# A graph network on one core: target degrees from run ends by rounds of eight largest keys, and loads of edge ends in three pieces

## The reference

```
h   = relu(layernorm(x))
x   = x + gnn(h)        # message = mlp(h[src], edge_attr), averaged over the edges of a target, then a second mlp
h   = relu(layernorm(x))
x   = x + propagate(h)  # ten steps; feat0 = h
    f   = f * clip(out_deg, 1)**-0.5
    agg = segment_sum(f[src], dst)
    f   = 0.9 * agg * clip(in_deg, 1)**-0.5 + 0.1 * feat0
```

## Time and profile before

| | us |
|---|---|
| three runs: lowest, median, highest | 8115.39, 8118.78, 8119.13 |
| profiled execution, its own time | 8119.95 |
| its span, first to last instruction | 8118.4 |
| TensorE (PE) busy | 5850.0 (72%) |
| VectorE (DVE) busy | 4429.2 (55%) |
| GpSimd (POOL) busy | 1670.8 (21%) |
| ScalarE (ACT) busy | 737.9 (9%) |

### The profile page before, as it was taken

The page is one execution under the profiler, slowest core; times in us unless marked ns, Lnnn a source line. Parts: engine busy times, 40 slices in busy tenths (PEclk is TensorE's granted clock), DMA queues, the critical chain, the costliest instruction groups (busy, mean ns, idle before and its releaser), DMA issues. The chain is left out here.

```text
span 8118.4 us, 215578 instructions
## 1 busy us (share of the span) xinstructions
PE 5850.0 (72%) x86684; PEld 3701.6 (46%) x86684; DVE 4429.2 (55%) x12772; ACT 737.9 (9%) x1743; POOL 1670.8 (21%) x1737
## 2 busy tenths in 40 slices
PE   5924444444444444443879999999999999999998
PEld 4723333333333333332435465556554655555555
DVE  4744444444444444443376666666666666666665
ACT  0012222222222222221100000000000000000000
POOL 0044444444444444445000000000000000000000
PEclk9986666666666666666589999999999999999999
DMA  2022222222222222221045555555555555555554
GB/s 80 0 66 60 60 60 64 60 60 61 62 60 60 60 60 60 63 60 51 4 180 193 201 191 199 193 201 191 200 193 201 192 201 193 193 197 198 202 193 173
DMA packets 442509, 1013.57 MB, mean 125 GB/s; under 512 B 253086, under 2 KB 371838, under 8 KB 387262
## 3 DMA queue, kind: packets, MB, share of 16 engines
q1 hardware_dynamic: 386878, 968.76, 33.6%
q0 software_dynamic: 54912, 33.89, 2.3%
HBM read 838.71 MB, written 176.58 MB: 125 GB/s over the span
## 5 line engine op out<-in xcount | busy, mean ns | idle before, releaser
L1529 PE MATMUL banks_fast<-count_units_fast,feature_parts_fast 128*32 128x512 fp8e3 x70608 | 3823.6, 379 | 50.3 <-DVE count_units_fast L1424 46.4
L1529 PEld LDWEIGHTS banks_fast<-count_units_fast,feature_parts_fast 128*32 128x32 bf16 x70608 | 2048.6, 97 | 1801.9 <-issue 54.1
L1423 DVE TENSOR_SCALAR count_units_fast<-packed_ring_fast 128x512 int32<-128x512 int32 x2949 | 1257.8, 427 | 1424.1 <-PE banks_fast L1529 1391.4
L858 POOL DMA_INDIRECT rows_fast<-row_table,idx_fast x1568 | 1508.8, 962 | 968.1 <-DVE idx_fast L939 489.8
L1117 PE MATMUL banks_fast<-w1a_b1a_fast,turn_fast 49*128 49x96 f32 x3136 | 372.5, 374 | 1815.5 <-ACT turn_fast L1028 1589.2
L1424 DVE TENSOR_SCALAR count_units_fast<-packed_ring_fast 128x512 int32<-128x512 int32 x2949 | 1240.3, 421 | 0.0
L1117 PEld LDWEIGHTS banks_fast<-w1a_b1a_fast,turn_fast 49*128 49x128 f32 x3136 | 293.3, 259 | 1913.7 <-ACT turn_fast L1028 1499.6
L963 DVE TENSOR_TENSOR window_src_hot_fast<-iota_by_windows_fast,window_keys_fast 128x1024 bf16<-128x1024 bf16 x392 | 270.3, 690 | 1585.5 <-PE banks_fast L1089 920.7
L967 DVE TENSOR_SCALAR window_place_hot_fast<-iota_wide_fast,local_keys_fast,target_weight_fast 128x196 bf16<-128x196 f16 x3136 | 929.7, 335 | 0.0
L1083 PE MATMUL banks_fast<-window_place_hot_fast,window_src_hot_fast 128*128 128x196 bf16 x3136 | 685.9, 310 | 43.9 <-issue 21.2
L1089 PE MATMUL banks_fast<-window_place_hot_fast,window_src_hot_fast 128*128 128x196 bf16 x3136 | 662.6, 303 | 0.0
(11 more groups left out here) (241 smaller groups left out, 1934.2 us busy)
## 6 DMA issues: line engine op xcount, KB each, us to landing
packed_ring_fast<-edge_counts SPq DMA_DIRECT2D x422, 1792.0 KB, 7.2
edge_counts<-count_stage_fast SPq DMA_DIRECT2D x100, 784.0 KB
running_sums<-run_sums_fast SPq DMA_DIRECT2D x100, 768.0 KB
rows_fast<-row_table,idx_fast POOLq DMA_INDIRECT x1568
rows_fast<-attrs_padded SPq DMA_DIRECT2D x98, 128.0 KB
attrs_padded<-in_edge_attr SPq DMA_DIRECT2D x1, 12500.0 KB, 41.2
row_table<-h_nodes_fast SPq DMA_DIRECT2D x1, 1568.0 KB, 5.2
edge_keys<-keys_fast SPq DMA_DIRECT2D x1, 1568.0 KB, 5.1
```

The costliest lines, as they stand in the source:

```text
L858: pool.indirect_dma_start(out=rows[:, s, c, 0:DN], out_offset=None, in_=b.dram.table, in_offset=bass.IndirectOffsetOnAxis(ap=idx[:, s, c:c ...
L1423: nc.vector.tensor_scalar(to[..., 0:P // 8], of, NIBBLES, None, ALU.bitwise_and)
L1529: last = nc.tensor.matmul(b.banks[at:at + DN, SWEEP[m % 2], 0:COLS], parts[:, side, j, k * DN:(k + 1) * DN], of_strip.bitcast(FP8), start= ...
```

## The change

Setup loads each of `src` and `dst` in three pieces: rows 0 to 111, 112 to 126 and 127.

```diff
-        LOADS = 17
+        LOADS, EVEN = 19, 112
...
-                sp.dma_start(tile[0:P - 1, :], ends[0:(P - 1) * T].rearrange("(p t) -> p t", t=T)).then_inc(loaded, 16)
+                for lo, hi in ((0, EVEN), (EVEN, P - 1)):
+                    sp.dma_start(tile[lo:hi, :], ends[lo * T:hi * T].rearrange("(p t) -> p t", t=T)).then_inc(loaded, 16)
                 sp.dma_start(tile[P - 1:P, 0:EL], ends[(P - 1) * T:E].rearrange("(p t) -> p t", p=1)).then_inc(loaded, 16)
```

```diff
+def sorted_degrees(nc, b, edges, overfull):
+    PIECES, ROUNDS, TOP = 4, 4, 8
+    W, KEPT = T // PIECES, ROUNDS * TOP
+    LIST, SPAN = PIECES * KEPT, 512
...
+        iota_wide = sb("iota_by_columns", [P, P, G], FP16)
+        part_hot, place_hot = sb("part_hot", [P, 2, P, G], FP16), sb("place_hot", [P, 2, J, G], FP16)
+        edge_hot = sb("edge_hot", [P, 2, J, G], FP16)
...
+        @block.gpsimd
+        def _(pool):
+            nc.gpsimd.iota(position[:, :].rearrange("p (c w) -> p c w", c=PIECES), pattern=[[0, PIECES], [1, W]], base=1,
+                           channel_multiplier=0).then_inc(counted_off, 1)
...
+            step(nc.vector.tensor_copy(iota_wide[:, :, :], b.iota16[:, :].unsqueeze(2).broadcast_to([P, P, G])))
+            step(nc.vector.scalar_tensor_tensor(out=node[:, :], in0=edges.dst_place[:, :], scalar=float(P),
+                                                in1=edges.dst_part[:, :], op0=ALU.mult, op1=ALU.add))
+            step(nc.vector.tensor_tensor(ends[:, 0:T - 1], node[:, 1:T], node[:, 0:T - 1], ALU.not_equal))
+            step(nc.vector.memset(ends[:, :].rearrange("p (c w) -> p c w", c=PIECES)[:, :, W - 1:W], 1.0))
+            step(nc.vector.tensor_scalar(key[:, :], node[:, :], first, float(SPAN), ALU.subtract, ALU.mult))
+            dve.wait_ge(counted_off, 1)
+            step(nc.vector.tensor_tensor(key[:, :], key[:, :], position[:, :], ALU.add))
+            step(nc.vector.tensor_tensor(key[:, :], key[:, :], ends[:, :], ALU.mult))
+            for r in range(ROUNDS):
+                for c in range(PIECES):
+                    piece, best = key[:, c * W:(c + 1) * W], top[:, c * KEPT + r * TOP:c * KEPT + (r + 1) * TOP]
+                    if r:
+                        dve.wait_ge(replaced, (r - 1) * PIECES + c + 1)
+                    nc.vector.max(out=best, in_=piece).then_inc(topped, 1)
+                for c in range(PIECES):
...
+                    dve.wait_ge(topped, r * PIECES + c + 1)
+                    nc.vector.match_replace(out=piece, in_to_replace=best, in_values=piece, imm_value=0.0).then_inc(replaced, 1)
+            dve.wait_ge(replaced, ROUNDS * PIECES)
+            step(nc.vector.tensor_reduce(overfull[:, :], key[:, :], AX.X, ALU.max))
...
+            for g in range(LIST // G):
+                s, of = g % 2, slice(g * G, (g + 1) * G)
+                dve.wait_ge(used, g + 1)
+                nc.vector.tensor_tensor(part_hot[:, s, :, :], iota_wide[:, :, :], part16[:, of].unsqueeze(1).broadcast_to([P, P, G]),
+                                        ALU.is_equal).then_inc(hot, 1)
+                nc.vector.tensor_tensor(place_hot[:, s, :, :], iota_wide[:, 0:J, :], place16[:, of].unsqueeze(1).broadcast_to([P, J, G]),
+                                        ALU.is_equal).then_inc(hot, 1)
+                dve.wait_ge(hot, 3 * g + 2)
+                nc.vector.tensor_tensor(edge_hot[:, s, :, :], place_hot[:, s, :, :], edges16[:, of].unsqueeze(1).broadcast_to([P, J, G]),
+                                        ALU.mult).then_inc(hot, 1)
...
+        @block.tensor
+        def _(pe):
+            pe.sem_inc(used, 2)
+            for g in range(LIST // G):
+                pe.wait_ge(hot, 3 * (g + 1))
+                for c in range(G):
+                    last = nc.tensor.matmul(count[:, 0, 0:J], part_hot[:, g % 2, :, c], edge_hot[:, g % 2, :, c],
+                                            start=(g == 0 and c == 0), stop=(g == LIST // G - 1 and c == G - 1))
+                last.then_inc(used, 1)
+            pe.wait_ge(used, LIST // G + 2)
+            pe.sem_inc(summed, 1)
```

In `prepare_sorted` two steps of one column make `overfull` a part of the flag, and two of 98 columns bound the starts and the ends of runs:

```diff
+            step(nc.vector.tensor_scalar(overfull[:, :], overfull[:, :], 0.0, None, ALU.is_gt))
+            step(nc.vector.tensor_tensor(unsorted[:, :], unsorted[:, :], overfull[:, :], ALU.max))
...
+            step(nc.vector.tensor_scalar(start[:, :], start[:, :], 0.0, float(E), ALU.max, ALU.min))
...
+            step(nc.vector.tensor_scalar(last[:, :], last[:, :], float(EP - 1), None, ALU.min))
```

More of the change, by code:

```diff
@@ L650, in prepare_sorted @@
 def prepare_sorted(nc, b, edges, ins, kept):
-    same, cont, last_row, window_row, unsorted = kept
+    same, cont, last_row, window_row, unsorted, overfull = kept
     with ExitStack() as ctx:
@@ L1622, in fast_way @@
         unsorted = ctx.enter_context(nc.sbuf_tensor("unsorted", [P, 1], FP32))
+        overfull = ctx.enter_context(nc.sbuf_tensor("overfull", [P, 1], FP32))
         with ExitStack() as edge_ctx:
@@ L1628, in fast_way @@
             setup(nc, b, edges, ins)
-            degrees(nc, b, edges, 1)
+            sorted_degrees(nc, b, edges, overfull)
             layer_norm_relu(nc, b, "in")
             store_table(nc, b, b.h)
-            prepare_sorted(nc, b, edges, ins, (same, cont, last_row, window_row, unsorted))
+            prepare_sorted(nc, b, edges, ins, (same, cont, last_row, window_row, unsorted, overfull))
             messages_and_counts(nc, b, edges, same, window_row, tail, counted_edges, crowded)
```

51 lines of the change are left out of this document (added).

## The result

The changed kernel takes 7826.45 us, the median of four runs (7824.22 to 7827.28), for 8118.6 of the kernel before: a ratio of 0.9641 (0.9624 to 0.9657), 292 us less. The forecast was 7830, the range 7815 to 7872. The profiled execution spans 7824.7 us, 293.7 less than before.

A forecast was written before the change was run, and what follows sets the result against it. Stages run one after another: setup's loads bound by one DMA engine of sixteen, the degree stage by its number of matmuls. -55.0 - 234.6 + 0.9 = -288.7 us from 8118.78 gave 7830 us, range 7815 to 7872.

The forecast's parts named there:

- Part 1: Setup's loads of the ends: three pieces an array let VectorE start at 30.0 in place of 84.97 us, -55.0 us.
- Part 2: Degree stage: the old path of 294.6 us is replaced by VectorE steps of 60.0 us, -234.6 us.
- (a): Degree stage, wide iota and making of the keys on VectorE: 10.5 us.
- (b): Degree stage, four rounds of eight-largest and match-and-replace over 392 columns on VectorE: 16.5 us.
- (c): Degree stage, a reduction over 1568 columns, 1.8 us, and twelve small steps over 128 columns, 3.8 us.
- (d): Degree stage, eight groups of three one-hot tiles on VectorE, with TensorE's matmuls beneath: 24.2 us.
- (e): Degree stage's end, the last group's matmuls and the way to the copy at L302: 3.2 us.
- Part 3: Preparation: two added one-column steps and two of 98 columns, all on the path, +0.9 us.
- The slow clock: Rival in the degree stage: TensorE at 1.2 GHz, its matmul pace halved, +23 us, 7853; chance 0.06.
- The dear max: Rival in the degree stage: max or replace is no plain stream, up to 68 us more, 7898; chance 0.07.
- the rhythm: Rival in the message loop: its 49 rounds change their beat, +76 us (7906) or -16 (7814); chance 0.07.
- The fallback: Rival: a piece with over 32 run ends makes the general way run too, +607 us, 8437; chance 0.03.

The follow-up runs named there:

- run 3: The changed kernel with the first two load pieces cut at 113 and 14 rows in place of 112 and 15: 7872.0 us, one run.
- runs 1 and 2: The kernel before with only the three-piece loads: 8059.7 us; the changed kernel with the ends loaded in two pieces as before: 7876.77 us.
- run 5: The changed kernel with the loads of ends issued first and x last: 6563.49 us, for 6861.67 of the kernel before on that faster chip.
- runs 10 and 11: The changed kernel with VectorE's wide iota moved behind the keys: 7822.43 us; the changed kernel with POOL's iota of positions moved into setup: 7820.26 us.
- run 8: The changed kernel with three sets of one-hot tiles in place of two: 6576.89 us, one run, on the faster chip.
- run 6: The changed kernel with 150 matmuls of zeros on TensorE while VectorE makes keys: 6569.5 us, one run, on the faster chip.

## Why the prediction was right

**The bound.** Both steps that carried the forecast stood: one engine of sixteen drained the loads (run 3), and the number of matmuls set the degree stage. The stages follow one another, so their terms add (runs 1 and 2). That the parts together came within 0.8 us is in part luck: single terms were off by up to 2.3 us, either way. One reading was loose: the 3446 us called the message loop are a window of 3290 us of loop and 156 of what follows it.

**Part 1** came out at 54.55 for 55.0, by luck: two errors of some 2 us cancel. "I take 0.45 plus 0.04 between two" was too dear: SP's 17 loads, two of them pairs, took from 19.84 to 26.14, 0.37 each. "The last load lands 2.0 us after its issue" was too cheap: 4.2 us passed from the end of the last issue to 30.34. The row I took for it, the L162 store, had nothing in front. Here the ends' own bytes stood ahead, moved until 28 at 225 GB/s, and 2.4 us more passed to 30.42. My upper bound had them at the pace of `x`, 151 GB/s, and so ending at 30.3. That number was hit by chance, since they moved faster and the wait behind them made up for it; but its idea, that the ends' bytes set the end and not the sum of issues, was right (run 5). The copy of the attributes cost nothing: it was issued at 32.30 and lay beside VectorE's work.

**Part 2, (a)** was mis-sized twice: "the wide iota is one L287, 1.23" measured 2.50, held by POOL's iota (runs 10 and 11), and the key step, for which I took 1.79 of L967's pattern, was 1.04, near my lower end. I had looked at whether POOL's iota would be in time, not at what it does to its neighbour. **(b)** 0.47 a max and 0.53 a replace with its load of values, for 0.48 and 0.55; the law through L750 and L714 held, and the reciprocal's rate as upper end was far off. **(c)** 0.27 a small step on average for 0.32. **(d)** That TensorE's 16 matmuls "fit beneath it, but only just" is the step that failed, by 1.1 us, of which run 8 gives back 1.0. **(e)** 3.36 for 3.2.

**Part 3.** That the added steps are "all on the path" and that "the block's own wait for the keys' store is behind them either way" was wrong, by 0.6 us. The store issued at 157.35 lands after VectorE has done its last step, and it ends the block. The two clamps of 98 columns shorten only the wait in front of the loop's first fill, 2.03 us for 2.53. The two one-column steps, in front of the store, are on the path.

**The rivals.** The slow clock: not excluded as I argued it. My "both at 1.00" was no evidence, since the column reads 1.00 over matmuls at the 1.2 GHz pace too (run 6). Of my two explanations the first held as far as the pace goes, which is the same at both levels; that it is the strided read of the weights that sets it, no run tests. The dear max, the loads and the rhythm did not come; the loop's times in the nine profiles at this speed other than that of before lie 6.5 us apart. The 76 us that I allowed were themselves too many: they start from rounds of 66.41 us, and 3290.3 / 49 is 67.15, from which all rounds at 67.96 would cost about 40. The fallback was not taken, but my price of 607 us, two stages of it alone, was low by a factor of 280.

## What to carry to other kernels

Look for stretches where no engine works and the DMA share is a sixteenth, and then at the number of rows of the transfers in it: cut at a multiple of 16, as here at 112 (0.97), and not at 113 (0.07). Before a list of one-hot matmuls is made faster, ask whether fewer columns would do, since here the stage's time was the count of matmuls and nothing else. When an added step on POOL lies beside a fast VectorE copy, put it where VectorE waits.

## What the runs showed of the hardware

- A copy of 2048 two-byte elements a row on VectorE takes 1.23 us alone and 2.50 when it starts with POOL's iota of 1.45 us; a step with two fp32 inputs is not held, 1.79 us either way (runs 10, 11). The Trainium skill ("GPSIMD Engine Reference", "1. Specifications") has POOL and VectorE contend for their access to SBUF when VectorE runs in a 2-port mode or with two SBUF inputs. The held copy agrees with the first; the second does not show here, beside a POOL step that has no input and only writes, and no run has one that reads.
- On VectorE the eight largest of 392 fp32 columns come every 0.47 us, (53.27 - 51.39) / 4, and a match-and-replace is a record of 0.55 to 0.60 with a separate record of 0.07 to 0.13 for the eight values.
- 98-column matmuls with both operands read at a stride of 16 elements keep 184 to 186 ns at a recorded clock of 1.00 and 0.50, and PEclk reads 1.00 where plain matmuls of 512 columns are still 427 ns apart (run 6).
- The same program, the kernel before, takes 8118 us on two chips and 6862 on a third. The difference is the message loop (3290 us for 2110) and the sums of nodes (317 for 243), whose code no run edits; the faster figures are those of run 5, since the kernel before has no profile there. All behind them takes the same (4059.5 and 4057.5). ScalarE's waits in the loop show where, first the kernel before on the slower chip, from 500 to 3700 us, then run 5 on the faster, from 200 to 2200 (us in total, times, longest):

```profile
ACT count_stage_fast L1023 <- remote: 1122.4, 95, 18.3
...
ACT run_sums_fast L1032 <- remote: 442.4, 41, 15.3
```

```profile
ACT turn_fast L1157 <- PE banks_fast L1229: 732.2, 190, 9.5
ACT count_stage_fast L1152 <- PE banks_fast L1212: 487.5, 390, 2.0
```

  On the slower chip ScalarE waits for something that the profile gives to no instruction ("remote"), on the faster one for nothing of the kind. By the code, ScalarE waits in each round for SP's stores of the sums and of the counts to DRAM, so these are the likely ones; no run tests it.
